# Issuing the rows of maxima from ScalarE instead of SyncE, a few steps behind their transpose

## The reference, cut to what matters

```
attn = q @ k * scale + rel_h + rel_w          # per head, per window
attn = softmax(attn)                          # exp(attn - rowmax) / sum
out  = attn @ v ; x = shortcut + out @ proj_w + proj_b
x    = x + gelu(ln(x) @ w1 + b1) @ w2 + b2
```

## Time and profile before

| | us |
|---|---|
| three runs | 702.13, 702.83, 706.59 |
| median of them | 702.83 |
| the profiled execution, whole | 705.98 |
| its span, from first to last instruction | 704.1 |
| TensorE busy in the span | 598.3 (85%) |
| VectorE / ScalarE / GpSimd busy | 294.2 / 220.0 / 129.5 |
| mean granted TensorE clock | 0.88 of full |

### The profile page before, as it was taken

One profiled execution on the slowest core, in us unless ns is written; L12 is line 12 of the kernel. 1 busy time (PEld: TensorE's weight loads), 2 busy tenths in 40 slices (PEclk: granted clock), 3 DMA queues, 4 the chain that ended last, 5 costly groups with the idle time before them and its releaser, 6 DMA issues.

```text
span 704.1 us, 9808 instructions
## 1 busy us (share of the span) xinstructions
PE 598.3 (85%) x3668; PEld 436.3 (62%) x3668; DVE 294.2 (42%) x817; ACT 220.0 (31%) x430; POOL 129.5 (18%) x185
## 2 busy tenths in 40 slices
PE   3986776898999989798987899989777767989997
PEld 1555655575666667465755686666477455836767
DVE  3356456535122353244543534134555556430123
ACT  2313325343233124143341324132134244241120
POOL 5402001003003213050440116003020011030011
PEclk9996586769999999799999899998955967799999
DMA  7781423052313345507346124301905230220001
GB/s 179 178 194 22 101 54 77 2 145 64 85 37 92 74 94 126 113 1 166 69 99 141 31 88 110 82 18 35 191 2 114 45 71 3 70 57 1 0 1 45
DMA packets 21829, 54.11 MB, mean 77 GB/s; under 512 B 4643, under 2 KB 10523, under 8 KB 21687
## 3 DMA queue, kind: packets, MB, share of 16 engines
q1 hardware_dynamic: 21782, 53.50, 33.4%
HBM read 10.94 MB, written 0.79 MB: 17 GB/s over the span
## 4 chain that ended last, share of the span: by engine, by line
PE 64%; DVE 11%; SPq 10%; DMA 7%; issue 4%; ACT 4%; DVEq 0%; ACTq 0%
PE PS L1141 61%; DMA QA<-NR 6%; SPq L707 4%; DVE NM L1037 3%; SPq L697 3%; PE PS L1153 2%; SPq L689 2%; SPq L719 1%; ACT REL L880 1%; DVE REL L1024 1%; DVE HL L1050 1%; DVE STAT L958 1%; DVE QHL L1005 1%; ACT HT L921 1%; ACT PT L900 1%
## 5 line engine op out<-in xcount | busy, mean ns | idle before, releaser
L1037 DVE TENSOR_REDUCE NM<-PS 98x2 f32<-98x392 f32 (+2 forms) x192 | 106.1, 570 | 128.4 <-PE PS L1141 127.2
L1141 PE MATMUL PS<-QA,KA 128*98 128x196 f32 (+2 forms) x480 | 109.9, 356 | 41.5 <-DMA QA<-NR 34.7
L900 ACT ACTIVATE PT<-PS 98x392 f32<-98x392 f32 (+2 forms) x192 | 93.5, 518 | 105.7 <-PE PS L1141 102.1
L1141 PEld LDWEIGHTS PS<-QA,KA 128*98 128x98 f32 (+2 forms) x480 | 85.4, 234 | 61.1 <-DMA QA<-NR 38.0
L1141 PE MATMUL PS<-KA,QA 126*98 126x196 f32 (+3 forms) x432 | 101.0, 340 | 13.8 <-DVE NM L1037 8.6
L1141 PEld LDWEIGHTS PS<-KA,QA 126*98 126x98 f32 (+3 forms) x432 | 72.2, 215 | 33.1 <-issue 14.0
L1141 PE MATMUL PS<-XT,WQKV 96*96 96x512 f32 x128 | 67.9, 664 | 4.3 <-issue 3.3
L1141 PE MATMUL PS<-XT,W 96*128 96x512 f32 x144 | 66.9, 620 | 3.4 <-issue 3.4
L1141 PE MATMUL PS<-PT,V 128*32 128x196 f32 (+2 forms) x672 | 58.8, 406 | 0.0
L810 POOL TENSOR_TENSOR OT<-XNOS,OT 128x512 f32<-128x512 f32 x18 | 22.9, 1276 | 187.1 <-DVE OT L1074 187.1
L1024 DVE TENSOR_TENSOR REL<-PS,REL 32x512 fp32r<-32x512 f32 (+5 forms) x64 | 28.8, 480 | 60.9 <-ACT REL L880 60.9
(11 more groups left out here) (88 smaller groups left out, 649.3 us busy)
## 6 DMA issues: line engine op xcount, KB each, us to landing
QA<-QHL SPq DMA_DIRECT2D x36, 192.0 KB
KA<-KHL SPq DMA_DIRECT2D x24, 228.0 KB
QA<-REL SPq DMA_DIRECT2D x24, 224.0 KB
QA<-QHL SPq DMA_DIRECT2D x12, 384.0 KB
KA<-KHL SPq DMA_DIRECT2D x12, 384.0 KB
KA<-PT SPq DMA_DIRECT2D x12, 380.0 KB
W<-in_w SPq DMA_DIRECT2D x6, 576.0 KB, 5.6
QA<-REL SPq DMA_DIRECT2D x24, 128.0 KB
```

What stands on the lines that cost most here:

```text
L900: nc.scalar.activation(dst, src, ACT.Exp).then_inc(probs_done.sem, 1)
L1037: nc.vector.tensor_reduce(dst, src, AX.X, ALU.max, negate=True).then_inc(max_done.sem, 1)
L1141: return nc.tensor.matmul(dst, lhsT, rhs, start=start, stop=stop, skip_group_check=loose)
```

## The change

Three edits. A function `with_rows` goes over the list of a layer's attention and puts a new step `rows h` behind each `maxT h`: at the latest right ahead of `scores h 0`, else once more than three steps have been put out behind `maxT h` (by its count four other steps then stand between). SyncE's part of `maxT` is taken away. ScalarE gets the part for `rows`: the same wait for the copy to `NR`, the same DMAs, the same semaphore.

```diff
--- before.py
+++ after.py
@@ -369,6 +369,19 @@
     return out
 
 
+def with_rows(steps, lag):
+
+    out, waiting = [], []
+    for step in steps:
+        while waiting and (len(out) - waiting[0][1] > lag or step[:3] == ("scores", waiting[0][0], 0)):
+            out.append(("rows", waiting.pop(0)[0], 0, 0))
+        out.append(step)
+        if step[0] == "maxT":
+            waiting.append((step[1], len(out)))
+    assert not waiting
+    return out
+
+
 def attention_steps(L):
 
     n = L.index
@@ -376,7 +389,7 @@
 
     if n == 0:
         out += [("ln", 0, 0, 0), ("turn", 0, 0, 0), ("ln", 0, 1, 0)]
-    out += windowed_attention(L) if L.pads else whole_attention(L)
+    out += with_rows(windowed_attention(L) if L.pads else whole_attention(L), 3)
     out += [("proj", t, 0, t) for t in range(6)]
     out += [("proj", t, 1, t) for t in range(4)] + [("ln", 1, 0, 0)] + [("proj", t, 0, t) for t in (6, 7)]
     out += [("proj", t, 1, t) for t in range(4, TILES)] + [("turn", 1, 0, 0), ("ln", 1, 1, 0)]
@@ -705,18 +718,6 @@
                              (m["QA"][L.rel_row:L.mask_row, 1, s, :], m["REL"][i::L.per_chunk, 1, :])]
                 for dst, src in moves:
                     sp.dma_start(raw(dst), raw(src)).then_inc(aug_in[s].sem, 16)
-            elif step == "maxT":
-
-                s, p = h % L.ring, h % 2
-                row = m["QA"][L.max_row:L.rows, L.tiles - 1, s, :]
-                sp.wait_ge(*maxT_done.at(n, h))
-                if L.pads:
-                    moves = [(row[:, 0:FIRST_EDGE], m["NR"][0:4 * NB, p, 0:HALF_IN]),
-                             (row[:, FIRST_EDGE:], m["NR"][4 * NB:, p, :])]
-                else:
-                    moves = [(row, m["NR"][:, p, :])]
-                for dst, src in moves:
-                    sp.dma_start(raw(dst), raw(src)).then_inc(max_row_in[p].sem, 16)
             elif step == "weights":
 
                 for wait in chunk_read(L, L.chunks - 1):
@@ -898,6 +899,18 @@
                     dst, src = m["PT"][:, h % 2, k % 2, (k // 2) * 512:(k // 2 + 1) * 512], PS[:, bank, :]
                 act.wait_ge(*scores_psum.at(n, j))
                 nc.scalar.activation(dst, src, ACT.Exp).then_inc(probs_done.sem, 1)
+            elif step == "rows":
+
+                s, p = i % L.ring, i % 2
+                row = m["QA"][L.max_row:L.rows, L.tiles - 1, s, :]
+                act.wait_ge(*maxT_done.at(n, i))
+                if L.pads:
+                    moves = [(row[:, 0:FIRST_EDGE], m["NR"][0:4 * NB, p, 0:HALF_IN]),
+                             (row[:, FIRST_EDGE:], m["NR"][4 * NB:, p, :])]
+                else:
+                    moves = [(row, m["NR"][:, p, :])]
+                for dst, src in moves:
+                    nc.scalar.dma_start(raw(dst), raw(src)).then_inc(max_row_in[p].sem, 16)
             elif step == "copy_o":
                 act.wait_ge(*pv_done.at(n, (i + 1) * L.per_group // L.pv_heads * L.pv_steps - 1))
                 if i:
```

## The result

The changed kernel takes 708.51 us (median of 20 runs, 700.82 to 713.25), the kernel before, run beside it, 702.15 us (20 runs): the ratio is 1.007, 95% interval 1.0044 to 1.0096, so the change costs about 0.7%, or 4.9 us. Ratios here leave out executions over 1.5% slower than the fastest of their kernel (five of the 20 after the change, the profiled one among them), so they differ a little from the ratios of the medians. The forecast was 686. In the kernels of this study the first copy to `NR` comes anywhere between 46.9 and 50.6 us, though all but one (e10) have the same code up to there, so from here on I compare the lengths of stretches, not times from the start.

What follows compares the result with a forecast made beforehand. TensorE was busiest, stopped most by the landing of rows of maxima (14 waits, 34.7 us). Layer 1's 12.7 plus 4.0 from two windowed layers, 16.7 us off the median 702.83, gave 686; range 676 to 700.

Steps and rivals of the forecast that it cites:

- Layer 1, 12.7 forecast: Layer 1: 11.0 us gained from TensorE's gaps and 1.7 from the clock, 12.7 in all.
- The gaps: Layer 1: TensorE's waits for rows and `aug`, 12.0 us, go but for 1.0: 11.0 gained, lower end 6.6.
- The clock: Layer 1: half clock from 292.5 to 299, after idle 3.26, mostly comes back: 1.7 us, between 0 and 2.0.
- Windowed layers, +2.0 each forecast: Layers 0 and 2: terms of heads 0, 3, 4 and the Exps sum to 2.0 us gained each, between -6.7 and 4.3.
- Heads 7 and 8 have no `aug` near: 0.: Windowed layers, heads 7 and 8: no `aug` copies near their rows, so no gain or loss, 0.
- Head 3, +1.0.: Windowed layers, head 3: row issued earlier, but `aug 8` beside it; 1.0 us gained, from -1.0 to 1.6.
- Head 4, -0.5.: Windowed layers, head 4: row already issued at once, `aug 9` now beside it; 0.5 us lost, from 0 to -1.9.
- Head 0, +2.0: Windowed layers, head 0: row issued earlier from ScalarE's queue, nothing in front; 2.0 us gained, between 0 and 2.7.
- ScalarE is held: Rival, windowed layers: rows go out behind finished Exps and delay Exps, 6.7 us lost a layer; 709.6 us, chance 0.06.
- Rows still land with the bulk: Rival, all layers: only issue time is saved, layer 1 gains 6.6, windowed layers lose 4.0; 700 us, chance 0.13.
- The clock stays up in the windowed layers too: Rival, windowed layers: the half clock after head 0's idle time goes, 4 us a layer; 678 us, chance 0.14.
- another wait steps in: Rival, layer 1: VectorE's maxima or the `aug` chain leave half of the 12.7 and of the 4.0; 694.5 us, chance 0.12.

Runs made afterwards that it cites:

- e10: e1 with `aug 7` moved right behind `maxT 3` and `aug 5` right behind `maxT 0` in the windowed layers; 684.87 us, ratio 0.9743.
- e1: The change kept to layer 1: there ScalarE issues the rows, in layers 0 and 2 SyncE does as before; 682.93 us, ratio 0.9763.
- e11: e1 run once more, unchanged, in a later job; 682.62 us, ratio 0.974.
- e5: The changed kernel, but SyncE's loads of the MLP's weights and what follows wait until head 11's row has landed; 697.12 us, ratio 0.9967.
- e4: The changed kernel, but in layers 0 and 2 SyncE waits at `maxT` until that head's row has landed; 691.98 us, ratio 0.9888.
- e7: e4 with the step `rows` right behind `maxT` in the windowed layers, not up to four steps later; 685.63 us, ratio 0.9789.
- e8: e1, but SyncE issues `aug 11` of layer 1 only once the row of head 9 has landed; 686.85 us, ratio 0.9801.

## Why the prediction was wrong

**Layer 1, 12.7 forecast: right, and 15.7 in the changed kernel.** Row 2 goes out as soon as its copy is there, and its wait is gone; so are 0.91 and 3.20, and SyncE's q and k copies of `aug 6` (307.68, 313.54) come 14 and 8 us ahead of its relative terms (321.76), where "5 us ahead" was forecast. Two terms were mis-sized, in opposite directions. The gaps gave 8.9, not 11.0, because the "rest at head 9" is 2.79 and not 0.6: `aug 11` is around that row. The clock gave 6.4, not 1.7 (9.3 in e1): I had priced one stretch of 17 matmuls behind one wait. That stretch is gone, though from 287 to 299 the changed kernel has slices of 4 us at 0.78, 0.50 and 0.87 where the kernel before has one at 0.57 (282 to 286). Read in the same slices, the kernel before also falls below the full clock from 382 to 398 (0.82, 0.75, 0.68, 0.90), behind its waits of 3.20 and 2.15, where the changed kernel has two such slices (0.72, 0.85), and once at 258 to 262 (0.57), which the changed kernel hasn't. This last is not shown to be the change's: e1 hasn't it and e11, the same kernel, has.

**Windowed layers, +2.0 each forecast: wrong, -8.6 and -10.5.** Four steps failed; the sizes are those of layer 0.

*"Heads 7 and 8 have no `aug` near: 0."* In fact -2.70 and -0.88, and -1.38 at head 6, 5.0 together. I had looked for the next `aug` in SyncE's list and not for whatever comes next there. What comes next, once the rows of heads 7 to 11 are out of that queue, is the step `weights`. e5 shows it: holding these loads alone gives 7.2 us back. At heads 3 and 4 the prediction asks what SyncE, freed of the row, issues beside it; it asks that of `aug` steps only.

*Head 3, +1.0.* In fact -2.1 (3.43 to 5.53), beyond the -1.0 that the range of this term held. The forecast took the 1.67 of an unloaded row and 0.6 for the bulk beside it. It took 5.11. The bulk was also put too low: a head's three copies in a windowed layer are 192, 228 and 224 KB by the page of the kernel before, 644 in all and not 384, which is one copy of layer 1.

*Head 4, -0.5.* The mechanism named (`aug 9` beside the row) was right; it cost 2.0, just beyond the -1.9 that the range of this term held.

*Head 0, +2.0, "since in ScalarE's own queue nothing is in front of it".* In fact 0.2. In front of the row stood the output copies of the projections (L872). The copy to `NR` was done at 50.8, and the row went out at 52.88, together with the start of the ACTIVATE in front of it. This is the second failed reason: that ScalarE's "sequencer runs ahead of the engine, so a DMA there does not wait until the unit in front of it is done". It does run ahead of the engine. Row 10 of the changed kernel stands behind the first Exp of head 9 in ScalarE's program, and went out 1.3 us before that Exp began:

```profile
145.00 0.62 ACTq L913 DMA_DIRECT2D QA<-NR  x1
...
146.27 0.54 ACT L901 ACTIVATE PT<-PS 98x392 f32<-98x392 f32 x1
```

But it did not pass an ACTIVATE that still waited for TensorE: rows 0, 3 and 7 went out as the one in front, its data come, began (52.88 and 52.88, 82.33 and the last Exp of that run, 118.89 and 118.87). Behind its copy to `NR` the row went out 2.1 us late at head 0, 0.6 at head 3 and 0.8 at head 7; at heads 4 and 8 it went at once.

That rival ("ScalarE is held") had 0.06, and it is part of what happened: with SyncE's next bulk held until the row has landed, e4's windowed stretches are still 5.7 us longer than e1's, and e7 shows that taking the lag away doesn't bring them back. Its number, 709.6, is the nearest of all to the 708.51 measured, but by luck: it had layer 1 gain 6.6 (15.7 in fact) and the windowed layers lose 13.4 (19.1), most of it, 3.8 a layer, for Exps behind the row, while in the changed kernel TensorE's waits for Exps grew by 1.2 us in all (6.7 to 7.9).

**Of the rivals** the one nearest in mechanism was "Rows still land with the bulk", 700 with 0.13. Row by row it is right: from the end of its issue row 9 took 1.3 us alone and 4.9 to 5.0 beside `aug 11`, and row 3 of e4 and of e1 took about the same from the end of the bulk's issue until TensorE went on (83.10 to 87.33, and 78.38 to 82.40), though the one was in ScalarE's queue and the other in SyncE's. But its time was too low in the windowed layers, since it left the old order of bulk in place, and too high in layer 1, for which it had 6.6. "The clock stays up in the windowed layers too" did not come: 0.67 went to 0.71 in layer 0 and 0.69 to 0.64 in layer 2. Nor did "another wait steps in": over the span no other wait of TensorE grew by more than those 1.2 us. The Trainium skill, "DMA: Bandwidth & Descriptors", section "Issuing engines are not separate DMA queues", says that the DMAs of both interleave on the same DMA engines, and the runs agree (5.11 us for row 3 beside SyncE's `aug 8`). I had set against it, from the section "Queues, rings and completion order" of that page of the Trainium skill, that each queue has its own ring served in turn. The same section also says that a DMA's semaphore write lands only after every earlier write of its DMA engine, across the queues; I had used half of it. Read whole, it would have a row wait for the bulk in front of it from either queue, and e4 and e8 agree as far as they go: row 3 in e4, behind `aug 7`, took as long as e1's, and row 9 in e8, with nothing beside it, 1.3 us.

**What stays open.** What issuing from ScalarE costs in the windowed layers was not taken apart head by head: the windowed stretches of e4 and e7 are both about 6 us longer than e1's, with the lag and without it. Whether a small row is late because its packets wait or because its completion does, no run here tells apart.

## What to carry to other kernels

A wait in a DMA queue does two things: it delays what is behind it, and it keeps that work from colliding with the DMA in front. Before taking a wait out, write down everything behind it in that queue up to the next wait, weight loads at the end of the layer included, and ask at what time each would now go out and beside which small urgent transfer; here a second queue gave no priority, while order in one queue and a wait for the landing did. And apply such a move stretch by stretch: the same edit was worth -17 us in one layer and +23 in the other two.

## What the runs showed that I had not expected

- A DMA issued by ScalarE stood behind an ACTIVATE that waited for TensorE, though its own data were ready 2 us and more before (2.1 at head 0; 3.6 at head 1 of layer 1 in e1), and went out as that one started (52.88 and 52.88; 118.89 and 118.87; in layer 1 327.55 and 327.52). Behind one that waited only for its turn on the engine it did not (145.00 and 146.27). With nothing between, it went 0.03 us after the copy (e7).
- An 8 KB copy on chip landed 1.3 us after its issue when it was alone (e8). With one head's bulk of layer 1 around it TensorE went on 5.5 us after the issue began when ScalarE issued it (364.73 to 370.24 in e1), and with that bulk in front 5.3 when SyncE did (385.57 to 390.88 before).
- In layer 1 the granted clock rose from 0.94 to 0.99 (e1; 0.98 in e11) when most waits of TensorE there went, and gave about as much time as the waits themselves: 9.3 us of 18.7 (7.5 of 16.8).
- Adding a wait made the kernel faster twice (e5 by 7.2 us, e4 by 12.8, against the changed kernel).
- Two executions of one kernel (e1 and e11) reached the first copy to `NR` 3.5 us apart, so a few us between two whole times may lie where the edit isn't.
